# Attention's steps in another order on four engines of one core

## The reference, cut to what matters

```python
x = x + 0.5 * _L0_ffn_ref(_layernorm(x), router_w, w1, w2, bias)
x = x + _L0_attn_ref(_layernorm(x), w_qkv, w_gated, w_proj, gn_weight, gn_bias)
x = x + 0.5 * _L0_ffn_ref(_layernorm(x), router_w, w1, w2, bias)
# attention, 16 heads of 16 channels
q, k = _rope_xpos(q, k, Tx)                                   # rotation
scores = einsum('bhtd,bhsd->bhts', q, k) * HEAD_DIM ** (-0.5)
scores = scores * mask[None]                                  # causal, gamma ** (t - s)
y = einsum('bhts,bhsd->bhtd', scores, v)
# y is normalised per head over channels and all tokens of its batch, then
out = silu(x @ w_gated.T) * yn;  return out @ w_proj.T
# experts: the two best of 8 per token, first CAP tokens of each expert in order of token
```

## Time and profile before

| | us |
|---|---|
| median of 3 runs | 2320.48 (2319.22 to 2325.01) |
| the profiled execution | 2339.04, its span 2337.2 |
| first expert stage ends, attention's first rows | 902.9, 913.6 |
| attention's batches begin (first `memory`) | 935.9, 994.4, 1059.0, 1134.6, 1210.8, 1288.1, 1364.3, 1441.6 |
| busy in the whole span: PE, DVE, ACT, POOL | 2165.9, 1362.6, 987.9, 1163.2 |
| mean granted TensorE clock | 0.965 |

### The profile page before, as it was taken

One profiled execution on the slowest core, in us unless ns is written; L12 is line 12 of the kernel. 1 busy time (PEld: TensorE's weight loads), 2 busy tenths in 40 slices (PEclk: granted clock), 3 DMA queues, 4 the chain that ended last, 5 costly groups with the idle time before them and its releaser, 6 DMA issues.

```text
span 2337.2 us, 57530 instructions
## 1 busy us (share of the span) xinstructions
PE 2165.9 (93%) x22289; PEld 1907.2 (82%) x22289; DVE 1362.6 (58%) x3363; ACT 987.9 (42%) x2173; POOL 1163.2 (50%) x911
## 2 busy tenths in 40 slices
PE   7869999999999997998899889839999999999998
PEld 6759999999999986776777677638899999999997
DVE  7755555555555543578777777655455555555553
ACT  4434444444444432455545554433344444444442
POOL 5755777644444433223333443365777745454443
PEclk9999999999999998999999989859999999999999
DMA  9523444444434424101212120234444444444432
GB/s 365 204 80 68 105 86 106 91 96 89 97 88 97 88 51 131 40 21 58 76 40 59 59 76 22 60 95 125 104 84 100 93 102 90 95 90 95 90 79 32
DMA packets 169414, 212.01 MB, mean 91 GB/s; under 512 B 50732, under 2 KB 147568, under 8 KB 165104
## 3 DMA queue, kind: packets, MB, share of 16 engines
q1 hardware_dynamic: 111888, 140.24, 18.0%
q0 software_dynamic: 57344, 69.21, 17.6%
HBM read 138.39 MB, written 73.14 MB: 91 GB/s over the span
## 4 chain that ended last, share of the span: by engine, by line
PE 50%; DVE 6%; issue 3%; ACT 1%; POOL 0%; another core or an unknown queue 0%; POOLq 0%; DMA 0%; DVEq 0%; ACTq 0%
PE bank L695 16%; PE bank L677 15%; PE bank L797 10%; PE bank L885 2%; PE bank L918 1%; PE bank L868 1%; PE bank L664 1%; PE bank L853 1%; PE bank L903 1%; PE bank L815 1%; DVE aw L1798 1%; DVE dl L1505 0%; DVE gsm L1854 0%; DVE rt L1786 0%
## 5 line engine op out<-in xcount | busy, mean ns | idle before, releaser
L1132 ACT ACTIVATE h<-bank 128x512 f32<-128x512 f32 x512 | 306.0, 598 | 853.8 <-PE bank L677 719.6
L1702 DVE CAST hh<-h 128x512 fp32r<-128x512 f32 x512 | 239.9, 468 | 695.9 <-ACT h L1132 582.5
L695 PE MATMUL bank<-w2h,hh 128*128 128x256 f32 x2048 | 579.2, 283 | 3.1 <-ACT yb L1150 3.1
L695 PE MATMUL bank<-w2l,hh 128*128 128x256 f32 x2048 | 573.8, 280 | 0.0
L695 PE MATMUL bank<-w2h,hl 128*128 128x256 f32 x2048 | 573.7, 280 | 0.0
L695 PEld LDWEIGHTS bank<-w2h,hh 128*128 128x128 f32 x2048 | 385.1, 188 | 45.5 <-ACT yb L1150 3.6
L695 PEld LDWEIGHTS bank<-w2h,hl 128*128 128x128 f32 x2048 | 384.8, 188 | 41.6
L695 PEld LDWEIGHTS bank<-w2l,hh 128*128 128x128 f32 x2048 | 385.2, 188 | 39.7 <-issue 0.3
L677 PE MATMUL bank<-xh,w1h 128*128 128x512 f32 x1024 | 405.2, 396 | 5.8 <-issue 5.1
L677 PE MATMUL bank<-xh,w1l 128*128 128x512 f32 x1024 | 404.5, 395 | 0.0
L677 PE MATMUL bank<-xl,w1h 128*128 128x512 f32 x1024 | 404.1, 395 | 0.0
(11 more groups left out here) (218 smaller groups left out, 3299.2 us busy)
## 6 DMA issues: line engine op xcount, KB each, us to landing
stg<-in_L_ffn_w SPq DMA_DIRECT2D x64, 1024.0 KB
xb<-acc SPq DMA_DIRECT2D x9, 1024.0 KB, 5.5
xa<-in_L_attn_x SPq DMA_DIRECT2D x8, 1024.0 KB, 14.2
xn_rows<-xa SPq DMA_DIRECT2D x8, 1024.0 KB
xn_rows<-xn_r SPq DMA_DIRECT2D x8, 1024.0 KB
xr<-acc SPq DMA_DIRECT2D x7, 1024.0 KB
out_rows<-xr SPq DMA_DIRECT2D x7, 1024.0 KB
slot_table<-pay,idx POOLq DMA_INDIRECT x256
```

The lines of the kernel that those rows point to most:

```text
L695: product = pe.matmul(tile_sum(j, t, end), a[:, fj, t * P:(t + 1) * P], c[:, fj, :], start=(fj == 0 and i == 0 and (end or t % 2 == 0)), s ...
L1132: act.activation(h32[fj % 2][:], bank[fj % 2][:], ACT.Gelu_apprx_tanh).then_inc(f.gelu, 1)
L1702: dve.tensor_copy(hh[:, fj, :], h32[fj % 2][:]).then_inc(f.hh, 1)
```

## The change

No instruction is added, removed or resized. In `sequence(b)` of PE, DVE, ACT and POOL the steps stand in another order, and `BANK_FILLS` follows PE's. The DMA queue of SP is as before. The core of the diff:

```diff
@@ POOL, sequence(b): its end
                 rotated(n + 8)
                 residual_power(b - 1)
+                half_bias(b - 1, 0)
+                rotated(n + 9)
+                first_output(b)
+                half_bias(b - 1, 1)
                 slots(b - 2, 0)
-                rotated(n + 9)
-                half_bias(b - 1, 0)
-                half_bias(b - 1, 1)
@@ PE, sequence(b): its start
+                project_values(n + 1)
                 scores(n, 0)
-                project_values(n + 1)
                 project(n + 2)
-                scores(n, 1)
                 turn(n + 1)
                 memory(n)
+                scores(n, 1)
+                scores(n + 1, 0)
                 new_state(n + 1, 0)
                 head_means(b - 1)
+                project(n + 3)
+                head_variances(b - 1)
+                turn(n + 2)
                 attend(n)
...
@@ ACT, sequence(b)
-                output(n + 3)
                 queries(n + 5)
                 front_norm(b + 1, 0)
+                gate(b, 2)
                 front_norm(b + 1, 1)
+                output(n + 3)
...
@@ DVE, sequence(b): its start
+                front_stats(b + 1, 0)
+                residual_choices(b - 2)
+                channel_stats(n - 1)
                 mask(n, 0)
-                channel_stats(n - 1)
-                residual_choices(b - 2)
-                front_stats(b + 1, 0)
                 channels(b - 1)
                 mask(n, 1)
...
```

More of the change, by code:

```diff
@@ L981, in sequence @@
                 new_state(n + 2, 1)
+                turn(n + 3)
                 scores(n + 2, 1)
-                project_values(n + 3)
-                turn(n + 3)
+                counts(b - 2)
                 memory(n + 2)
-                counts(b - 2)
+                gate(b, 0)
                 attend(n + 2)
-                gate(b, 0)
+                project(n + 5)
+                turn(n + 4)
+                scores(n + 3, 0)
                 new_state(n + 3, 0)
-                project(n + 5)
-                scores(n + 3, 0)
-                turn(n + 4)
+                project_values(n + 4)
+                new_state(n + 3, 1)
                 memory(n + 3)
-                new_state(n + 3, 1)
                 scores(n + 3, 1)
-                project_values(n + 4)
                 gate(b, 1)
                 out_tile(b - 1, 0)
+                new_state(n + 4, 0)
+                attend(n + 3)
                 scores(n + 4, 0)
-                attend(n + 3)
-                new_state(n + 4, 0)
-                scores(n + 4, 1)
+                new_state(n + 4, 1)
                 out_tile(b - 1, 1)
@@ L1959, in sequence @@
+                carry(n + 2, 0)
                 front_stats(b + 1, 2)
[L1960 to L1966 removed]
                 mask(n + 2, 0)
[L1968 to L1969 removed]
                 places(b - 2, 0)
                 gating(b - 1, 0)
+                places(b - 2, 1)
@@ L1995, in sequence @@
+                channel_stats(n)
+                front_low(b + 1, 0)
+                mask(n + 5, 0)
+                residual(b - 1, 2)
+                residual_stats(b - 1, 1)
+                carry(n + 5, 0)
                 places(b - 2, 4)
-                carry(n + 5, 0)
-                rotate(n + 7)
-                residual(b - 1, 2)
+                residual(b - 1, 3)
+                channel_stats(n + 1)
                 slot_entries(1, b - 2)
-                residual_stats(b - 1, 0)
@@ L2001, in sequence @@
-                front_low(b + 1, 0)
-                carry(n + 5, 1)
-                mask(n + 5, 0)
-                residual(b - 1, 3)
-                residual_stats(b - 1, 1)
-                residual_stats(b - 1, 2)
-                channel_stats(n + 1)
                 channel_stats(n + 2)
                 mask(n + 5, 1)
+                rotate(n + 7)
+                residual_stats(b - 1, 2)
+                carry(n + 5, 1)
                 residual(b - 1, 4)
+                carry(n + 6, 0)
```

138 lines of the change are left out of this document (65 added, 73 removed).

## The result

The changed kernel takes 2332.05 us (median of 8 runs, 2325.56 to 2336.91), the kernel before 2320.61 us in the same series (2319.22 to 2325.01): a ratio of **1.0045**, 95% interval 1.0028 to 1.0061. I had forecast 2282.0 and a range of 2262 to 2314. The profiled execution took 2336.66 us, its span is 2334.8. The prediction is wrong by 50 us and in its sign.

What follows compares the result with a forecast made beforehand. PE, nearest to full in attention, was taken as the bound, losing time to waits and low clock. Gains of 2.5 + 4.5 = 7.0 us times 5.5 batches took 2339.0 to 2300.5, less 18.6 for profiling 2282.0 us; range 2262 to 2314.

Steps and rivals of the forecast that it cites:

- Waits of a full batch: PE's idle time per attention batch: 2.1 us at the start for 3.5, 1.0 at `counts` for 2.1; gain 2.5 us.
- The clock: PE's low clock in a full batch: one short stretch of 1.7 us in place of 6.2, gain 4.5 us.
- Rival 2: PE in attention: the low clock stays as it is, gain 14 us, 2306.5 us; chance 0.25.
- rival 4: Batch start: `turn` waits on a ring through POOL's addition and ACT's norms; 8 us slower, 2328.5 us; chance 0.08.
- 7.0 us a batch: Gain per full attention batch, 2.5 us of waits plus 4.5 of clock; times 5.5 batches makes 38.5 us.
- the sum consists of waits and clock only: Attention, batches 2 to 7: nothing is added, so only PE's waits and clock were priced, 7.0 us a batch.
- batches 0 and 1 count nothing: First two attention batches: neither the slow `dl` nor a low clock there, so no gain or cost was counted.
- 18.6 us as the cost of profiling: Whole kernel: profiled execution's excess over the median, taken as belonging to profiling, so the forecast went from 2300.5 to 2282.0 us.
- The rule on signals: Batch start, the 0.91 us mask wait: lateness may belong to the products; 1.4 us a batch less gain, about 2290.
- rival 3: Attention: the waits only move, DVE becomes the bound in the first half; gain near 0, 2320 us; chance 0.10.

Runs made afterwards that it cites:

- the shift by 88: Changed kernel with 44 tiny transposes (88 instructions) more on PE in front of attention, where PE stands idle; 0.9916 of the kernel before, 2303.9 us.
- b_noload: Kernel before with the 1 MB loads of `xb` for batches 2 to 7 cut to their first tile (128 KB); 0.9982 of the kernel before.
- b_shift88: Kernel before with 44 tiny transposes (88 instructions) more on PE in front of attention; 1.0016 of the kernel before.
- b_shift200: Kernel before with 100 tiny transposes (200 instructions) more on PE in front of attention; 1.0038 of the kernel before.
- b_load4: Kernel before with each 1 MB load of `xb` sent as four of 256 KB; 0.9981 of the kernel before.
- b_shift128: Kernel before with 64 tiny transposes (128 instructions) more on PE in front of attention; 1.0000 of the kernel before.
- the runs without the loads: Changed kernel and kernel before, each with the `xb` loads for batches 2 to 7 cut to their first tile; 0.9952 and 0.9982 of the kernel before.

## Why the prediction was wrong, point by point

**Waits of a full batch, right.** Forecast 2.1 us at the start; measured 0.89 + 1.16 in the batch at 1379. At `counts` I had 0.45 and 0.55 us. In that batch neither is there, but a stop of 1.23 us inside `memory(n + 2)`, behind its first product of 32, is; it is a block border and not a wait:

```profile
1395.40 0.40 PE L955 MATMUL bank<-scn,cst 128*128 128x16 f32 x2
...
1395.95 0.24 PE L904 MATMUL bank<-qkT,state 32*32 32x64 f32 x1
1397.41 0.65 PE L904 MATMUL bank<-qkT,state 32*32 32x64 f32 x31 [1.23 <-issue]
```

**The clock, right where there is no stop.** One short stretch (0.59 from 1383 to 1387), 0.98 in the window. Rival 2 (the clock stays) is out for these batches, and rival 4 too: POOL's addition is on time, no `turn` waits for more than 0.9 us. But each long stop lowers the clock once more. Behind the stop at 1211 (1.00, 1.00, then 0.66):

```profile
1204.00:1208.00 4.00, 4.00 (x132) 3.17 (x130) 3.30 (x11) 1.11 (x3) 1.27 (x1) 1.00 0.52 152
1208.00:1212.00 4.00, 0.69 (x21) 0.51 (x13) 0.61 (x2) 0.22 (x1) 0.00 (x0) 1.00 0.34 114
1212.00:1217.00 5.00, 4.51 (x64) 3.73 (x62) 1.58 (x4) 2.04 (x6) 0.00 (x0) 0.66 0.01 3
```

**7.0 us a batch, right in the best batches, too large on the mean.** 77 us became 72 in the undisturbed batches and 70 in two of those with the shift by 88. From the start of batch 2 to the last `counts` that kernel takes 452.4 us where the profiled execution of before takes 487.3: 34.9 us less, forecast 38.5. But that execution was a long one (the third failure, below). Four others in that order (`b_noload`, `b_shift88`, `b_shift200`, `b_load4`) take 477.7 to 481.8 us for the same stretch (`b_shift128`, with its 10 stops, 486.9). Against the four it is 25 to 29 us, about 5 us a batch.

**The step that failed: "the sum consists of waits and clock only".** It took PE's stream of instructions as always there. In the two parts of attention, before and after:

```profile
928.70:1059.00 130.30, 126.22 (x3042) 99.47 (x3042) 86.47 (x233) 63.22 (x144) 30.68 (x25) 1.00 0.11 31
1059.00:1546.30 487.30, 418.86 (x8967) 334.27 (x8966) 364.54 (x1030) 236.26 (x473) 184.77 (x151) 0.89 0.20 61
```

```profile
921.90:1070.00 148.10, 139.49 (x3026) 108.52 (x3026) 89.28 (x239) 64.73 (x147) 30.45 (x25) 0.91 0.10 30
1070.00:1546.50 476.50, 410.80 (x8983) 326.36 (x8982) 366.05 (x1023) 232.40 (x470) 178.72 (x151) 0.93 0.20 62
```

From batch 2 on the changed kernel wins 10.8 us and not 38.5. Against the shifted kernel (452.4 us) it loses 24.1. Its idle time is 476.5 - 410.8 = 65.7 us against 44.1, thus 21.6 more, and what the profile lays to "issue" is 25.6 us against 5.4 of it, so the stops account for 20.2. That much is shown by runs in which only borders moved.

**The second failure: "batches 0 and 1 count nothing".** They cost 17.8 us (148.1 against 130.3). I had looked for waits that the change could remove there, found none, and not asked which it adds: the wait of `turn` for POOL and of the doubled `scores` for the mask, 0.9 us each, were in my own walk through the order and hold for every batch. Their part, with the clock that falls behind them, is about 8 us (in the runs without the loads batch 2 starts 138.0 us behind the first `turn` in the new order and 129.7 in the old); the rest is stops and the clock behind them (0.91 on the mean in place of 1.00, in the windows above).

**The third: 18.6 us as the cost of profiling.** Profiling costs no such sum: the profiled execution lies 4.6 us above the median for the changed kernel, and in the experiments from 10 us below it to 11 us above. The profiled execution of before was simply a long one: its first `turn` came at 928.7 where that of the changed kernel came at 921.9, and its attention took 617.6 us, where the three variants of before with about its number of stops took 607.4 to 611.9. The changed kernel's profiled execution missed its forecast by 2336.7 - 2300.5 = 36.2 us, the median by 50.0; the difference, 14 us, comes from here. The 36.2 us are the 27.7 that batches 2 to 7 missed and the 17.8 of batches 0 and 1, less some 9 by which this execution was faster outside of attention.

**The rule on signals** that I had weighed from the Trainium skill ("Perfetto Trace Analysis", Tensor Engine Instruction: a product's signal goes out when PSUM acknowledges the write), by which the wait of 0.91 us would come back, did not decide anything: the wait in question turned into the 1.16 us of the doubled `scores`, which stand behind a mask that DVE reaches only after its channel means (1380.62 in the rows above), and no late signal can be seen in that place.

None of my rivals named this mechanism. Rival 4 (2328.5) came nearest in time and has the right sign, by a cause that is not there: no `turn` waits for POOL for more than 0.9 us. That it came near is chance. Nor is rival 3 (2320) there: DVE was busy for 58 to 59 us a batch as before. The Trainium skill has the rule that could have warned me, with the opposite sign: "Runtime: NRT & Kernel Launch", Instruction fetch mechanics, says that each engine's instructions come through a queue of its own in blocks of 256, and that this is hidden, since instructions are issued more slowly than blocks come. The first half agrees with this trace (96 packets of 16 KB for 96 blocks). The second does not: an `attend` passes 128 instructions in 1.05 us, and PE stood still for 32.9 us at borders.

**What stays open.** I can't say what sends a block's packet. Without a transfer in the way it mostly started about 1 us after the border before (median 1.15 us in the changed kernel, 3.64 us with a transfer in the 3 us before it), yet some went out before that border and some 4 us behind it. The kernel with 512 more instructions had its borders at the same numbers and its long stops partly in other batches. Whether cutting the write of `out_rows` and the load of `xr` into pieces would take away the stops behind them was not tried. Nor was it tried what the dense runs would give if large products were set between them.

## What to carry to other kernels

Before pricing a change of order, count the dense stretches: where 256 instructions of PE pass in under some 3.5 us, or a transfer of 1 MB runs in front of such a stretch, an idle time "by issue" in the middle of a step may be the instruction stream, and its place moves with every instruction added or removed anywhere in front of it. So test a new order at two or three shifts (some idle instructions where the engine waits anyway) before judging it: here one order gave 0.992 to 1.005 of the old kernel by that alone. And when a step is moved, charge its new waits in every batch, also in those where it had nothing to remove.

## What the runs showed of the hardware that I had not expected

- PE's instructions come in packets of 16 KB, 256 instructions (96 packets for some 24,660 instructions in the changed kernel). Stops recur at one number modulo 256 and move with a shift by exactly that shift: 149 to 151, then 86 and 87 with 64 more, and 149 to 151 again with 512 more.
- The first instruction behind a border ran at the earliest 2.0 us after its packet's start; the stops ended 2.0 to 3.0 us after it, though the packet itself took 0.9 to 1.8 us.
- A packet that is wanted while a 1 MB transfer runs comes late. Behind loads and writes of 1 MB alike 18 packets of the changed kernel started 3.2 to 4.4 us into the transfer, from 1.9 us ahead of its last piece to just behind it; two more started in its first 1.4 us, none between. One stop took 3.31 us with the load and 0.84 us without it.
